# LSTM layer on one core: the bias of the turned gate sums is put back by copies instead of matmuls

## The reference

```python
xW = jnp.einsum('ntd,dg->ntg', x, Wx) + b
def step(carry, xw_t):
    prev_h, prev_c = carry
    a = xw_t + prev_h @ Wh
    i = jax.nn.sigmoid(a[:, :Hdim])
    f = jax.nn.sigmoid(a[:, Hdim:2 * Hdim])
    o = jax.nn.sigmoid(a[:, 2 * Hdim:3 * Hdim])
    g = jnp.tanh(a[:, 3 * Hdim:])
    next_c = f * prev_c + i * g
    next_h = o * jnp.tanh(next_c)
    return ((next_h, next_c), next_h)
...
x = x + lstm(x, cond, Wx, Wh, b)
ys = cond / 16
x = x + ((x * ys) @ w) * rsqrt((ys * ys) @ (w * w) + eps)
```

## Time and profile before

| | |
|---|---|
| median of 3 executions | 1943.04 us (1942.17 to 1943.12) |
| the profiled execution's own time | 1940.92 us |
| its span, first to last instruction | 1939.1 us |
| granted TensorE clock, mean | 0.996 |
| PE busy | 1739.9 us (90%) |
| PE weight loads busy | 1577.4 us (81%) |
| DVE busy | 1263.6 us (65%) |
| ACT busy | 886.4 us (46%) |
| POOL busy | 258.1 us (13%) |

### The profile page before, as it was taken

One profiled execution on the slowest core, in us unless ns is written; L12 is line 12 of the kernel. 1 busy time (PEld: TensorE's weight loads), 2 busy tenths in 40 slices (PEclk: granted clock), 3 DMA queues, 4 the chain that ended last, 5 costly groups with the idle time before them and its releaser, 6 DMA issues.

```text
span 1939.1 us, 303170 instructions
## 1 busy us (share of the span) xinstructions
PE 1739.9 (90%) x135928; PEld 1577.4 (81%) x135928; DVE 1263.6 (65%) x12825; ACT 886.4 (46%) x6148; POOL 258.1 (13%) x1295
## 2 busy tenths in 40 slices
PE   7989899999989898989999999889898989999998
PEld 7888888888888888888888888888888888888886
DVE  4666666666666666666666666666666666666665
ACT  2444444444444444444444444444444444444443
POOL 1111111111111111111111111111111111111110
PEclk8999999999999999999999999999999999999999
DMA  3000000000000000000000000000000000000001
GB/s 94 0 0 0 0 0 0 0 0 0 0 0 0 0 0 0 0 0 0 0 0 0 0 0 0 0 0 0 0 0 0 0 0 0 0 0 0 0 0 43
DMA packets 4444, 6.68 MB, mean 3 GB/s; under 512 B 1106, under 2 KB 2900, under 8 KB 4436
## 3 DMA queue, kind: packets, MB, share of 16 engines
q1 hardware_dynamic: 3872, 5.51, 0.9%
q10 hardware_dynamic: 564, 1.05, 0.2%
HBM read 4.46 MB, written 2.10 MB: 3 GB/s over the span
## 4 chain that ended last, share of the span: by engine, by line
PE 72%; ACT 15%; DVE 7%; issue 5%; DMA 0%; ACTq 0%
PE pA L221 24%; PE pS L235 15%; PE pB L235 14%; ACT tanhc L192 8%; ACT ogate L190 7%; DVE hst L384 7%; PE pA L228 6%; PE pA L207 6%; PE pA L201 6%; PE pA L322 1%; DMA bias_col<-in_bC_dram 0%; PE pB L213 0%; PE pS L313 0%; ACTq L173 0%; DVE ores L399 0%
## 5 line engine op out<-in xcount | busy, mean ns | idle before, releaser
L221 PE MATMUL pA<-wh_sb,hst 128*4 128x64 f32 (+2 forms) x24576 | 654.0, 220 | 180.0 <-DVE hst L384 177.9
L185 ACT ACTIVATE gates<-pB 128x8 f32<-128x8 f32 x2048 | 351.4, 184 | 1014.6 <-DVE pB L368 1006.1
L368 DVE STREAM_TRANSPOSE pB<-pA 128x64 f32<-128x64 f32 x2048 | 444.9, 263 | 449.4 <-PE pA L221 449.3
L221 PEld LDWEIGHTS pA<-wh_sb,hst 128*4 128x4 f32 (+2 forms) x24576 | 395.2, 87 | 295.4 <-DVE hst L384 292.8
L235 PE MATMUL pS<-hst,wh_sb 128*32 128x2 f32 x32768 | 509.7, 177 | 1.5 <-issue 1.5
L372 DVE CUSTOM_DVE_ANT_1 junk<-gates 128x4 f32<-128x4 f32 x4096 | 424.6, 160 | 113.8
L235 PE MATMUL pB<-hst,wh_sb 128*32 128x2 f32 x32768 | 465.0, 174 | 0.0
L235 PEld LDWEIGHTS pB<-hst,wh_sb 128*32 128x32 f32 x32768 | 430.6, 110 | 0.0
L143 POOL TENSOR_TENSOR xh<-xh,hst 128x4 f32 (+1 forms) x1024 | 206.9, 202 | 1652.1 <-DVE hst L384 1652.1
L235 PEld LDWEIGHTS pS<-hst,wh_sb 128*32 128x32 f32 x32768 | 423.9, 108 | 1.6 <-issue 1.6
L228 PE MATMUL pA<-wh_sb,hst 128*4 128x32 f32 (+3 forms) x16384 | 423.1, 193 | 0.0
(11 more groups left out here) (41 smaller groups left out, 295.5 us busy)
## 6 DMA issues: line engine op xcount, KB each, us to landing
outT_dram<-ores SPq DMA_DIRECT2D x8, 256.0 KB, 2.5
xh<-in_xT_dram SPq DMA_DIRECT2D x6, 320.0 KB
wh_sb<-in_Wh_dram ACTq DMA_DIRECT2D x1, 1024.0 KB, 8.1
wx_sb<-in_Wx_dram SPq DMA_DIRECT2D x1, 1024.0 KB, 7.6
w_sb<-in_w_dram SPq DMA_DIRECT2D x1, 256.0 KB, 6.7
xh<-in_xT_dram SPq DMA_DIRECT2D x2, 64.0 KB, 8.2
bias_sb<-in_bT_dram ACTq DMA_DIRECT2D x2, 1.0 KB
condT<-in_condT_dram ACTq DMA_DIRECT2D x1, 2.0 KB, 7.8
```

Source lines behind the costliest of these rows:

```text
L185: act.activation(gates[:, j, :, 0:2 * PAIR].rearrange("p b (q a) -> p a q b", a=PAIR), pB[:, j, :, 0:PAIR * Q].rearrange("p a (q r) -> p a ...
L221: last = pe.matmul(pA[j][c * Q:c * Q + M, 0:PAIR * Q].rearrange("p (g u) -> p g u", u=Q), hst[:, k, lo:lo + M], two(wh_sb[:, k, :], c, j, ...
L368: dve.transpose(pT[j][:, 0:PAIR * Q], pA[j][:, 0:PAIR * Q]).then_inc(turned_and_fsum_ready[j], 1)
```

## The change

The bias of the turned sums (gates i and g) no longer comes from matmuls. It is laid out on the host as `bR`, a full 128 x 2 x 64 tile that has the values as `pA` wants them, and loaded once into `bias_rows` (in place of a memset, two small loads and `bias_sb`). In s = 2 VectorE copies its first half into `pA[0]` (`reset_rows(0)`), after the two transposes, and ScalarE copies the second half into `pA[1]` with an activation of the function Copy, between `gates` and `ogate`. TensorE's `fill_x(j, ...)` waits for `rows_reset[j]` of its half; the wait for `gates_ready[1]` is gone there. `fill_bias` is gone. The numbers of fillers in s = 0 to 3 become 1, 1, 1, 2, where they were 0, 0, 0, 1. Ahead of the loop, `pA` is cleared by matmuls, one more filler follows the 32, and VectorE resets both halves once.

```diff
+    FILL = (1, 1, 1, 2)
...
-            act.wait_ge(bias_zeroed, 1)
-            for n, g in enumerate(TURNED):
-                act.dma_start(bias_sb[0:1, n * D:(n + 1) * D], bT[:, g * D:(g + 1) * D]).then_inc(bias_loaded, 16)
+            act.dma_start(bias_rows[:, :, :], bR).then_inc(bias_loaded, 16)
...
                         act.activation(gates[:, j, :, 0:2 * PAIR].rearrange("p b (q a) -> p a q b", a=PAIR),
                                        pB[:, j, :, 0:PAIR * Q].rearrange("p a (q r) -> p a q r", q=PAIR)[:, :, :, cols],
                                        ACT.Sigmoid).then_inc(gates_ready[j], 1)
+                    if t == T - 1:
+                        act.activation(pA[1][:, 0:PAIR * Q], bias_rows[:, 1, :], ACT.Copy).then_inc(rows_reset[1], 1)
...
-            def fill_bias(j):
-                for c in range(G):
-                    last = pe.matmul(pA[j][c * Q:(c + 1) * Q, 0:PAIR * Q].rearrange("p (g u) -> p g u", u=Q), picks[:, :],
-                                     two(bias_sb[:, :], c, j, 1), start=True, stop=False, skip_group_check=True)
-                return last
...
+            def clear(of):
+                for c in range(G):
+                    pe.matmul(of[c * Q:(c + 1) * Q, 0:PAIR * Q], picks[:, :], zeros[:, 0:PAIR * Q], start=True, stop=True)
+
+            def filler(count):
+                for _ in range(count):
+                    pe.matmul(pA[0][0:Q, P:2 * P], picks[:, :], zeros[:, :], start=False, stop=True, skip_group_check=True)
...
+            for j in range(K):
+                last = clear(pA[j])
+            filler(WARM)
+            pe.matmul(pA[K - 1][0:Q, P:2 * P], picks[:, :], zeros[:, :], start=False, stop=True,
+                      skip_group_check=True).then_inc(rows_cleared, 1)
...
             for j in range(K):
+                pe.wait_ge(rows_reset[j], 1)
                 for k in range(K):
                     last = fill_x(j, k)
...
+                        filler(FILL[s])
                     elif t == T - 1:
-                        pe.wait_ge(gates_ready[1], it * T + (s + 1))
                         for j in range(K):
-                            fill_bias(j)
-                        for j in range(K):
+                            pe.wait_ge(rows_reset[j], it + 2)
                             for k in range(K):
                                 last = fill_x(j, k)
                         last.then_inc(filled, 1)
+                        filler(FILL[s])
                     else:
                         pe.wait_ge(xh_ready, it * T + (2 * T - 1))
                         pe.wait_ge(gates_ready[0], it * T + (s + 1))
-                        filler(False)
+                        filler(FILL[s])
...
+            def reset_rows(j):
+                return dve.tensor_copy(pA[j][:, 0:PAIR * Q], bias_rows[:, j, :])
...
+            dve.wait_ge(bias_loaded, 16 * 2)
+            dve.tensor_scalar(bias_rows[:, :, Q:PAIR * Q], bias_rows[:, :, Q:PAIR * Q], 2.0, None, ALU.mult).then_inc(rows_doubled, 1)
+            dve.wait_ge(rows_doubled, 1)
+            dve.wait_ge(rows_cleared, 1)
+            for j in range(K):
+                reset_rows(j).then_inc(rows_reset[j], 1)
...
                         dve.transpose(pT[j][:, 0:PAIR * Q], pA[j][:, 0:PAIR * Q]).then_inc(turned_and_fsum_ready[j], 1)
+                    if t == T - 1:
+                        dve.wait_ge(turned_and_fsum_ready[0], it * (2 * T) + 2 * (s + 1))
+                        reset_rows(0).then_inc(rows_reset[0], 1)
```

More of the change, by code:

```diff
@@ L9, with build @@
 ALU = mybir.AluOpType
-def build(nc, xT_in, condT_in, Wx, Wh, bT, bC, w, outT):
+def build(nc, xT_in, condT_in, Wx, Wh, bR, bC, w, outT):
     D, B, SEQ = xT_in.shape
@@ L40, in build @@
         wh_sb = sb("wh_sb", [P, K, G * D])
-        bias_sb = sb("bias_sb", [P, PAIR * D])
+        bias_rows = sb("bias_rows", [P, K, PAIR * Q])
         bias_col = sb("bias_col", [P, PAIR * K])
@@ L72, in build @@
         out_written = [sem(f"out_written{n}") for n in range(2)]
-        bias_zeroed, buffers_zeroed, operands_ready = (sem(n) for n in (
-            "bias_zeroed", "buffers_zeroed", "operands_ready"))
+        buffers_zeroed, operands_ready = (sem(n) for n in ("buffers_zeroed", "operands_ready"))
         ys_ready, squares_ready, demod_summed, demod_added, demod_rooted, demod_ready, wmod_ready = (sem(n) for n in (
@@ L82, in build @@
         gates_ready = [sem(f"gates_ready{j}") for j in range(K)]
-        x_edged = sem("x_edged")
+        x_edged, rows_doubled, rows_cleared = (sem(n) for n in ("x_edged", "rows_doubled", "rows_cleared"))
+        rows_reset = [sem(f"rows_reset{j}") for j in range(K)]
         x_carried = [sem(f"x_carried{n}") for n in range(PAIR)]
@@ L122, in _ @@
         def _(pool):
-            pool.memset(bias_sb[:, :], 0.0).then_inc(bias_zeroed, 1)
             pool.memset(xh[:, :, :, 0:1], 0.0).then_inc(x_edged, 1)
@@ L237, in still @@
                 return last
-            def filler(start):
-                pe.matmul(pA[0][0:Q, P:2 * P], picks[:, :], zeros[:, :], start=start, stop=True, skip_group_check=True)
+            def clear(of):
[4 more added lines that the diff above has]
+                    pe.matmul(pA[0][0:Q, P:2 * P], picks[:, :], zeros[:, :], start=False, stop=True, skip_group_check=True)
             pe.wait_ge(zeros_ready, 1)
@@ L244, in _ @@
             for n in range(PAIR * K):
[L245 to L250, removed]
-            for j in range(K):
-                fill_bias(j)
+                clear(sums[n])
+            for j in range(K):
+                last = clear(pA[j])
+            filler(WARM)
+            pe.matmul(pA[K - 1][0:Q, P:2 * P], picks[:, :], zeros[:, :], start=False, stop=True,
+                      skip_group_check=True).then_inc(rows_cleared, 1)
+            pe.wait_ge(operands_ready, 2)
             pe.wait_ge(xp_ready, 1)
@@ L260, in _ @@
             last.then_inc(filled, 1)
-            pe.wait_ge(operands_ready, 4)
+            pe.wait_ge(operands_ready, 3)
             for n in range(PAIR):
@@ L342, in _ @@
             g_cols = slice(G_ * D, (G_ + 1) * D)
-            dve.wait_ge(bias_loaded, 16 * 3)
-            dve.tensor_scalar(bias_sb[0:1, D:PAIR * D], bias_sb[0:1, D:PAIR * D], 2.0, None, ALU.mult).then_inc(operands_ready, 1)
+            def reset_rows(j):
[6 more added lines that the diff above has]
+                reset_rows(j).then_inc(rows_reset[j], 1)
             dve.wait_ge(wx_loaded, 16)
@@ L416 @@
         "Wh": _np.ascontiguousarray(inputs["L0_cond_Wh"]),
-        "bT": _np.ascontiguousarray(_np.asarray(inputs["L0_cond_b"]).reshape(1, 4 * d)),
+        "bR": _np.ascontiguousarray(_np.repeat(_np.asarray(inputs["L0_cond_b"]).reshape(4, d // 128, 4, 32)[0::3].transpose(2, 1, 0, 3), 32, axis=0).reshape(128, d // 128, 64)),
         "bC": _np.ascontiguousarray(_np.asarray(inputs["L0_cond_b"]).reshape(4 * d // 128, 128).T),
```

## The result

The changed kernel takes 1910.4 us (median of 4, 1908.4 to 1910.7) against 1943.1 us: a ratio of 0.983, 95% interval 0.981 to 0.985. The profiled execution took 1910.27 us.

The account below looks back on a forecast made before the run. The loop through `hst` bounds three steps, TensorE's queue s = 2. From 1940.9 us, 23 gained in s = 2 and 0.5 lost at the start gave 1918.4; the median lies 2.1 above, so 1920.6 us, range 1911 to 1947.

Parts of the forecast that it names:

- ScalarE's copy: In s = 2, the copy into `pA[1]` starts at 5.68, lasts 0.255 us and ends at 5.935; `fill_x(1)` starts at 5.99.
- What bounds the kernel, and the most that can be won: Three steps set by the loop through `hst`, s = 2 by TensorE's queue; at most 0.13 us a body, 33 us.
- Reading `tanhc` as released by the cell and not by `ogate`: In s = 2 the first `tanhc` waits for the cell until 5.94, so the first `ogate` has 0.11 us to spare.
- The fillers: Each added filler holds TensorE 0.22 us: hidden in s = 0, 1 and 3, ahead of `turned` in s = 2.
- VectorE's copy: In s = 2, the copy into `pA[0]` takes 0.23 us from about 5.45, hidden with 0.05 to spare.
- D: Rival: VectorE's copy starts only at 5.57, `turned` at 6.515; no gain, about 1942 us; chance 0.07.
- the sum: For s = 2: `fill_x(1)` from 5.99 to 6.21, filler to 6.43; `turned` at 6.43 instead of 6.52, 23 us gained.
- A: The case as worked out: copy between 0.24 and 0.27 us gives 1916 to 1925 us; chance 0.50.
- B: Rival: `gates` hold ScalarE for 0.16 whatever follows, copy starts at 5.75; gain 5 us, 1938.4 us; chance 0.22.
- The range: For the whole kernel's time, 8 in 10 runs: 1911 to 1947 us.
- the full stall: The whole 0.13 us a body of s = 2 won, `hst` being the bound: gain 33 us, 1910 us.
- E: Rival: TensorE's clock falls, over 2% lost, or Copy needs its own function table, 655 us; chance 0.06.

Follow-up runs that it names:

- experiment 8: The changed kernel with one more 64-column copy on ScalarE, into an unused SBUF tile, between the reset and `ogate`: 1927.9 us, ratio 0.992.
- experiment 1: The changed kernel with two fillers instead of one in s = 2: 1964.2 us, ratio 1.011.
- experiment 9: The kernel before, bias matmuls kept, with `fill_bias(j)` waiting for `turned_and_fsum_ready[j]` and fillers 1, 1, 1, 2: 1953.8 us, ratio 1.006.
- experiment 6: The changed kernel with ScalarE's copy 128 columns wide instead of 64: 1922.7 us, ratio 0.990.
- experiment 4: The changed kernel with ScalarE's copy reading the bias from PSUM instead of SBUF, and an added wait ahead of VectorE's `carry_x(0)`: 1919.7 us, ratio 0.989.
- experiment 5: The changed kernel with an already met wait on `turned_and_fsum_ready[1]` ahead of ScalarE's copy: 1909.1 us, ratio 0.983.
- experiment 10: The changed kernel with the fillers of the kernel before, 0, 0, 0, 1: 1907.2 us, ratio 0.982.
- experiment 11: The changed kernel without any filler in the loop: 2042.2 us, ratio 1.050.
- Experiment 3: The kernel before, no copies, with `fill_bias(j)` waiting for `turned_and_fsum_ready[j]` instead of `gates_ready[1]`: 1909.2 us, ratio 0.983.
- experiment 2: The changed kernel without the filler in s = 2: 1908.6 us, ratio 0.983.

## Why the prediction was right, and where it was wrong

The mechanism was right, and the time fell outside the range: 1910.4 us against 1920.6 and a lower end of 1911. The step that failed is the term for ScalarE's copy into `pA[1]`. The prediction let it start 0.09 behind the second `gates` and last 0.255 us; it started 0.07 behind and lasted 0.228.

*What bounds the kernel, and the most that can be won.* Right. The stall of s = 2 was 0.13 us, and it went as a whole. (A bracket names `hst` before three of the four starts in the earlier trace rows, not two; the reading is the same.)

*Reading `tanhc` as released by the cell and not by `ogate`.* Right: `ogate` moved by 0.06 and `tanhc` did not move; pushed further in experiment 8, it did.

*The fillers.* Right in price (0.21 and 0.17 us in experiments 1 and 9, 0.22 and 0.17 expected) and in that three of them are hidden. That the filler in s = 2 would be what binds was wrong by a hair: it ties with `hst`. The prediction had the filler hold back the start of `turned`; experiments 1 and 6 show that it holds back one of four column groups and with it the transposes, at the same price.

*VectorE's copy.* Forecast 0.23 from 5.45, measured 0.214 starting 0.34 behind the first transpose, where I had 0.35. Right, and VectorE's own queue hides it. D didn't happen. But `fill_x(0)` starts on it and sets the earliest start of `fill_x(1)`: the sum had this path 0.035 us ahead of ScalarE's (5.955 against 5.99), measured it is 0.003.

*ScalarE's copy: the term that failed.* "Duration 0.205 + 0.05 = 0.255" measured 0.228, and "start 5.59 + 0.18 - 0.09 = 5.68", 0.09 behind `gates`, measured 0.07 to 0.08. Together 0.04 us: `turned` was forecast 1.86 behind the start of its step and came at 1.82, the moment at which `hst` allowed it. 256 x 0.04 = 10 us is the whole distance from 1920.6 to 1910.4. That the time stopped just there is in part luck: with the filler's path, the path of `hst` and VectorE's copy so close together, a still shorter copy would have brought nothing more. The slope was right (0.8 ns, experiment 6). The base was wrong: I took a `tanhc` of 0.205 as the price of any activation that reads SBUF, and the copy lasted as long from PSUM (experiment 4). Taking 0.8 ns a column off for 64 columns leaves 0.177, nearer to `ogate`'s 0.16 to 0.17 than to `tanhc`; why `tanhc` takes longer, no run shows. The estimate of 0.239 from the figure of the Trainium skill ("ScalarE: Activation LUTs", section "What ACT_TABLE_LOAD costs") was nearer by 0.016; it was weighed and set aside.

*The reason for choosing A over B* (only PSUM-reading neighbours are held for 0.16) was wrong though the choice was right: experiments 4 and 5 show no such hold, from either source, with or without a wait. The 0.16 was read as a hold, but is the distance of two releases (experiment 5).

*The range.* Its lower end should have been the full stall, for which the text itself had 1910 us; it was written as 1911. Since two paths ended 0.04 us apart in the sum, with the uncertain term only on the later one, the full stall deserved much more than a side remark in A.

*E.* The clock held, and no table was loaded in the loop (the traces of both kernels have the same two table loads, ahead of it and behind it). The reason given, that no gap grows, is in line with experiments 10 and 11, where only the widening of the gap in s = 3 made it fall. Whether one filler at another place would do as well was not tried.

*What nobody had listed.* The change was costed as an exchange of matmuls for copies. Experiment 3 shows that moving one wait takes away the whole stall; the reset itself could have stayed where it was. The copies pay only for the filler in s = 2 (experiment 9), and that filler brings nothing (experiment 2). The rows had it: `fill_bias` starts 0.06 behind the end of `gates` and 0.30 behind the end of the second transpose.

## What to carry to other kernels

Before work is moved off the engine that stalls, look at what its first instruction waits for, and whether it is the last reader of what it overwrites: here one wait for an engine that doesn't touch the buffer cost more (0.18 us) than the whole stall (0.13). When two paths end within the error of a term, give the time of the other path its full share in the range. Fillers are priced by where they stand: nothing in a gap, their full length where a critical matmul comes next (from the second filler on, here), and the last one left was worth 135 us, through the clock. Before a fixed distance between two instructions is read as a hold of the engine, look at what released the second.

## What the runs showed of the hardware that was not expected

- ScalarE's Copy of 64 columns into PSUM lasts 228 ns from SBUF and 226 ns from PSUM, and 279 ns at 128 columns; it starts 0.07 behind a `gates` of 0.184, an overlap of 0.11. An activation whose semaphore comes last starts 0.023 behind the semaphore's change (experiment 5).
- A second wait ahead of a VectorE operation came with 0.14 us although it had been met 0.09 us earlier (experiment 4); a single met wait on ScalarE cost nothing (experiment 5).
- A matmul in one column group and matmuls in the others run beside each other, and later ones can start first: at 4.38, ahead of a filler record that starts at 4.48 (experiment 1).
- Removing one filler of 0.22 us from each body of 7.3 us lets the granted clock fall to 0.84 to 0.86 on average, and the kernel becomes 7% slower than with it (experiments 10 and 11).
